# Bias rows, one-hot comparison and group additions redistributed in the edge loop of a two-layer graph network

## The reference, cut to what matters

```python
edge_feat = concatenate([x[src], x[dst], edge_attr], axis=-1)   # 20000 x 1088
h = mish(edge_feat @ W1 + b1)                                   # 20000 x 512
messages = mish(h @ W2 + b2)                                    # 20000 x 512
agg = segment_sum(messages, dst, num_segments=1250)
```

## Time and profile before

| | us |
|---|---|
| runs (3) | 1095.49, 1094.32, 1094.78 |
| median | 1094.78 |
| profiled execution, its own time | 1094.15 |
| its span | 1092.3 |
| busy: PE / weight loads / VectorE / ScalarE / GpSimd | 1033.1 / 871.1 / 861.9 / 884.3 / 724.6 |
| granted TensorE clock, mean | 0.986 |
| edge loop, from the first `z1` behind the node products to the last message | about 370 to 1020 |

### The profile page before, as it was taken

How to read it: one execution, slowest core, us unless ns; L and a number is a source line. 1 busy time by engine, 2 the same in 40 slices (tenths; PEclk the granted TensorE clock), 3 DMA queues, 4 the chain that set the end, 5 groups by cost and what they waited for, 6 DMA issues and landing times.

```text
span 1092.3 us, 18562 instructions
## 1 busy us (share of the span) xinstructions
PE 1033.1 (95%) x5629; PEld 871.1 (80%) x5630; DVE 861.9 (79%) x1500; ACT 884.3 (81%) x1077; POOL 724.6 (66%) x626
## 2 busy tenths in 40 slices
PE   3558999999999999999999999999999999999997
PEld 1226889998889888888888888888888888888796
DVE  7998536635526389999999999999999999999686
ACT  6985735624503799999999999999999999999584
POOL 6875438745255587777777777777777777760227
PEclk8889999999999999999999999999999999999999
DMA  2005962674276387766676666667766666761002
GB/s 106 9 1 139 181 222 73 212 242 149 77 240 116 94 177 163 162 161 139 136 147 139 139 141 146 136 141 141 147 137 138 144 146 134 142 133 39 1 1 95
DMA packets 82914, 141.63 MB, mean 130 GB/s; under 512 B 11115, under 2 KB 39020, under 8 KB 82742
## 3 DMA queue, kind: packets, MB, share of 16 engines
q0 software_dynamic: 38048, 87.58, 40.1%
q1 hardware_dynamic: 44822, 53.52, 15.3%
HBM read 115.42 MB, written 20.39 MB: 124 GB/s over the span
## 4 chain that ended last, share of the span: by engine, by line
PE 85%; DVE 7%; ACT 2%; issue 2%; POOL 1%; DMA 1%; DVEq 1%; ACTq 0%; POOLq 0%
PE banks L1149 12%; PE banks L1150 12%; PE banks L1154 12%; PE banks L1047 10%; PE banks L1181 7%; PE banks L1131 7%; PE banks L1124 6%; PE banks L1091 5%; PE banks L965 4%; PE banks L1112 4%; DVE edge_counts L1823 2%; PE banks L1244 2%; DVE key_onehot L1762 1%; PE banks L1020 1%; PE banks L1147 1%
## 5 line engine op out<-in xcount | busy, mean ns | idle before, releaser
L798 POOL DMA_INDIRECT gather_pq<-q_table,dst x157 | 326.1, 2077 | 57.2 <-issue 47.5
L790 POOL DMA_INDIRECT gather_pq<-p_table,src x157 | 174.8, 1113 | 117.7 <-PE banks L1131 66.7
L1149 PE MATMUL banks<-w_lo,h_hi 128*128 128x512 f32 x620 | 242.0, 390 | 0.0
L1150 PE MATMUL banks<-w_hi,h_hi 128*128 128x512 f32 x620 | 241.8, 390 | 0.0
L1154 PE MATMUL banks<-w_hi,h_lo 128*128 128x512 f32 x620 | 166.0, 389 | 0.0
L1154 PEld LDWEIGHTS banks<-w_hi,h_lo 128*128 128x128 f32 x620 | 116.4, 188 | 24.4
L1150 PEld LDWEIGHTS banks<-w_hi,h_hi 128*128 128x128 f32 x620 | 116.4, 188 | 23.8
L1149 PEld LDWEIGHTS banks<-w_lo,h_hi 128*128 128x128 f32 x620 | 116.4, 188 | 23.3 <-issue 0.7
L2131 DVE SCALAR_TENSOR_TENSOR h_full<-mish_work,banks 128x512 f32<-128x512 f32 (+1 forms) x154 | 98.4, 681 | 45.1 <-ACT mish_work L1465 40.8
L2156 DVE SCALAR_TENSOR_TENSOR message<-mish_work,banks 128x1024 f32<-128x1024 f32 x78 | 95.3, 1222 | 8.4 <-ACT mish_work L1489 0.3
L1124 PE MATMUL banks<-ident,gather_pq 128*128 128x128 f32 x628 | 96.5, 275 | 1.4 <-DVE h_full L2131 0.8
(11 more groups left out here) (274 smaller groups left out, 2607.6 us busy)
## 6 DMA issues: line engine op xcount, KB each, us to landing
edge_attr<-in_edge_attr_t SPq DMA_DIRECT2D x20, 256.0 KB, 2.8
attr_high<-edge_attr_hi SPq DMA_DIRECT2D x40, 128.0 KB, 2.2
attr_low<-edge_attr_lo SPq DMA_DIRECT2D x40, 128.0 KB, 1.8
edge_attr_parts<-attr_high SPq DMA_DIRECT2D x79, 64.0 KB
edge_attr_parts<-attr_low SPq DMA_DIRECT2D x79, 64.0 KB
x_nodes<-h_hi POOLq DMA_DIRECT2D x10, 256.0 KB, 14.9
x_nodes<-h_lo POOLq DMA_DIRECT2D x10, 256.0 KB, 7.9
p_table<-p_stage SPq DMA_DIRECT2D x10, 256.0 KB, 2.0
```

Of the source, the lines that this page charges most:

```text
L790: nc.gpsimd.indirect_dma_start(GP[:, 2 * j + k, :], None, p_tab[:, :], bass.IndirectOffsetOnAxis(ap=SRC[:, 2 * s + k:2 * s + k + 1], axis= ...
L798: nc.gpsimd.indirect_dma_start(GP[:, 2 * j + k, :], None, q_tab[:, :], bass.IndirectOffsetOnAxis(ap=DST[:, 2 * s + k:2 * s + k + 1], axis= ...
L1149: pe.matmul(at, h_high(s, j)[:, c, e], W2_LO[:, c, :], start=False, stop=False, skip_group_check=True)
L1150: pe.matmul(at, h_high(s, j)[:, c, e], W2_HI[:, c, :], start=False, stop=False, skip_group_check=True)
```

## The change

1. `b2_second_tile` of ScalarE is gone. In odd steps VectorE's `b2_rows` writes the row into both banks of the step with one copy of 128x1024; in even steps it writes the first bank as before, and TensorE adds the row in the second by the product with ones. In odd steps TensorE adds none. TensorE waits on one semaphore, counted once a step, ahead of k = 0.
2. `hots1` makes both one-hots with one `tensor_tensor` of 128x2x128 in place of two `tensor_scalar` of 128x128.
3. Of a group's two additions, the one to the lowest tile stays at the end of the even step; the one to the next tile moves to the following odd step, behind `full1` and ahead of `hi2`. `load_range` moves from the end of the even step to a place behind `message` in the odd step.

The order of VectorE in an odd step s is then: `full1(s)` twice, `group_next`, `hi2`, `hi1`, `lo2`, `message`, `load_range`, `hots1`, `b2_rows` (both banks), `lo1`.

```diff
--- before.py
+++ after.py
@@ -416,7 +416,7 @@
         z1_done, a_exp, a_sq, a_ln, a_r, h_hi, h_lo = (sem(n) for n in
             ("z1_done", "a_exp", "a_sq", "a_ln", "a_r", "h_hi", "h_lo"))
         h_full = [sem(f"h_full_{h}") for h in range(2)]
-        z2_done, b2_in, b2_first, b2_second = (sem(n) for n in ("z2_done", "b2_row_in", "b2_in_first_tile", "b2_in_second_tile"))
+        z2_done, b2_in, b2_in_rows = (sem(n) for n in ("z2_done", "b2_row_in", "b2_written"))
         b_exp, b_sq, b_ln, b_r, msg_full, msg_hi, msg_lo = (sem(n) for n in
             ("b_exp", "b_sq", "b_ln", "b_r", "msg_full", "msg_hi", "msg_lo"))
         u_bias, u_exp, u_cut, u_sq, u_ln, u_r, u_ready = (sem(n) for n in
@@ -1140,10 +1140,8 @@
                         pe.wait_ge(up_moved, BLOCKS * KD)
                     pe.wait_ge(h_hi, s + 1)
                 if after(s, 2) and k == 0:
-                    pe.wait_ge(b2_first, s - 1)
-                elif after(s, 2) and j == 0:
-                    pe.wait_ge(b2_second, s)
-                else:
+                    pe.wait_ge(b2_in_rows, s - 1)
+                elif not after(s, 2) or j == 0:
                     pe.matmul(at, ONES_R[:, :], B2_R[:, :], start=True, stop=False, skip_group_check=True)
                 for c in range(KD):
                     pe.matmul(at, h_high(s, j)[:, c, e], W2_LO[:, c, :], start=False, stop=False, skip_group_check=True)
@@ -1488,9 +1486,6 @@
                 act.wait_ge(b_ln, s + 1)
                 nc.scalar.activation(z2_work(s), z2_work(s), ACT.Exp, scale=-1.0).then_inc(b_r, 1)
 
-            def b2_second_tile(s, j):
-                nc.scalar.copy(Z2[:, 2 * j + 1, :], B2_ROW[:, 0, :]).then_inc(b2_second, 2)
-
             def edge_step(s, j):
 
                 if live(s):
@@ -1503,9 +1498,6 @@
                     inv1(s)
                 if live(s - 2):
                     sq2(s - 2)
-                if j == 1 and after(s, 3) and live(s - 1) and tiles(s - 1) == 2:
-                    b2_second_tile(s - 1, 1 - j)
-                if live(s - 2):
                     log2(s - 2)
                 if live(s - 2):
                     inv2(s - 2)
@@ -1527,7 +1519,6 @@
                             log1(s)
                         if n == first + 3:
                             inv1(s)
-            act.wait_ge(b2_in, 16)
             for s in range(2, 4):
                 edge_step(s, s % 2)
             with act.Fori(2, LAST - 1) as i:
@@ -1681,13 +1672,15 @@
             def node_tile(nt):
                 return AGG[:, bass.ds(nt, 1), :].rearrange("p o d -> p (o d)")
 
-            def add_sums(n, row, bank):
-
-                next_tile = dve.snap(range_regs[n][R_NEXT], min_val=0, max_val=NT - 1)
-                for nt, where in ((low_tile(n), FROM_LOW), (next_tile, BELOW_LOW)):
-                    at = node_tile(nt)
-                    ins = nc.vector.scalar_tensor_tensor(at, bank, where[:, bass.ds(row, 1)], at, ALU.mult, ALU.add)
-                return ins
+            def add_low(n, row, bank):
+
+                at = node_tile(low_tile(n))
+                nc.vector.scalar_tensor_tensor(at, bank, FROM_LOW[:, bass.ds(row, 1)], at, ALU.mult, ALU.add)
+
+            def add_next(n, row, bank):
+
+                at = node_tile(dve.snap(range_regs[n][R_NEXT], min_val=0, max_val=NT - 1))
+                return nc.vector.scalar_tensor_tensor(at, bank, BELOW_LOW[:, bass.ds(row, 1)], at, ALU.mult, ALU.add)
 
             def sums_extra(n, rel, tile, hots, bank, added):
 
@@ -2147,7 +2140,10 @@
 
             def hots1(s, j):
 
-                make_hots([ONEHOT[:, j, k, :] for k in range(2)], REL_G, 2 * s).then_inc(hot_ready, 1)
+                wide = [P, 2, P]
+                nc.vector.tensor_tensor(ONEHOT[:, j, :, :], IOTA[:, 0:P].rearrange("p (o k) -> p o k", o=1).broadcast_to(wide),
+                                        REL_G[:, bass.ds(2 * s, 2)].rearrange("p (t o) -> p t o", o=1).broadcast_to(wide),
+                                        ALU.is_equal).then_inc(hot_ready, 1)
 
             def message(s, j):
                 dve.wait_ge(b_r, s + 1)
@@ -2155,9 +2151,12 @@
                     dve.wait_ge(msg_lo, s)
                 nc.vector.scalar_tensor_tensor(MSG[:, :, :], EB[:, :, :], -0.5, z2_out(s, j), ALU.add, ALU.mult).then_inc(msg_full, 1)
 
-            def b2_first_tile(s, j):
+            def b2_rows(s, j):
                 dve.wait_ge(msg_full, s - 1)
-                nc.vector.tensor_copy(Z2[:, 2 * j, :], B2_ROW[:, 0, :]).then_inc(b2_first, 1)
+                if j == 1:
+                    nc.vector.tensor_copy(Z2[:, 2:4, :], B2_ROW[:, :, :].broadcast_to([P, 2, DIM])).then_inc(b2_in_rows, 1)
+                else:
+                    nc.vector.tensor_copy(Z2[:, 0, :], B2_ROW[:, 0, :]).then_inc(b2_in_rows, 1)
 
             def hi2(s):
                 dve.wait_ge(msg_full, s + 1)
@@ -2169,30 +2168,34 @@
                 dve.wait_ge(msg_hi, s + 1)
                 nc.vector.tensor_tensor(MSG_LO[:, :, :], MSG[:, :, :], MSG_HI[:, :, :].bitcast(F32), ALU.subtract).then_inc(msg_lo, 1)
 
-            def add_group(s, n, group, bank):
-
+            def group_low(s, n, group, bank):
 
                 wait_extras()
                 dve.wait_ge(agg_done, SUMS1 + group)
                 dve.wait_ge(seg_done, s + 1)
-                add_sums(n, group, bank).then_inc(agg_done, 1)
+                add_low(n, group, bank)
+
+            def group_next(s, group):
+
+                add_next(0, group, SEG[:, 0, :]).then_inc(agg_done, 1)
+                more_of(s, 0, group + 1)
+
+            def add_group(s, n, group, bank):
+
+
+                group_low(s, n, group, bank)
+                add_next(n, group, bank).then_inc(agg_done, 1)
 
             def more_of(s, n, added):
                 sums_extra(n, REL_G, 2 * s, [XHOT_R[:, k, :] for k in range(tiles(s))], SEG[:, 1, :], SUMS1 + added)
-
-            def sums1(s, group, last):
-
-                if last:
-                    add_group(s, 0, group, SEG[:, 0, :])
-                    more_of(s, 0, group + 1)
-                else:
-                    more_of(s, 0, group)
 
             def edge_step(s, j, i):
 
                 if live(s):
                     for h in range(2):
                         full1(s, h)
+                if j == 1 and live(s - 4):
+                    group_next(s - 4, i - 2)
                 if live(s - 3):
                     hi2(s - 3)
                 if live(s):
@@ -2201,16 +2204,19 @@
                     lo2(s - 3)
                 if live(s - 2):
                     message(s - 2, j)
+                if j == 1 and live(s - 3):
+                    load_range(0, i - 1)
                 if live(s - 2):
                     hots1(s - 2, j)
                     if live(s):
-                        b2_first_tile(s, j)
+                        b2_rows(s, j)
                 if live(s):
                     lo1(s, j)
                 if live(s - 3):
-                    sums1(s - 3, i - 2 + j, j == 0)
-                if live(s - 2) and j == 0:
-                    load_range(0, i - 1)
+                    if j == 0:
+                        group_low(s - 3, 0, i - 2, SEG[:, 0, :])
+                    else:
+                        more_of(s - 3, 0, i - 1)
 
             dve.wait_ge(q_stored, TABLE_STORED)
             dve.wait_ge(b2_in, 16)
@@ -2224,6 +2230,8 @@
                 edge_step(s, s % 2, s // 2)
 
 
+            group_next(FINAL - 3, EDGE_GROUPS - 3)
+            load_range(0, EDGE_GROUPS - 2)
             hi2(FINAL - 2)
             lo2(FINAL - 2)
             more_of(FINAL - 2, 0, EDGE_GROUPS - 2)
```

## The result

The changed kernel takes 1110.11 us in the median of 4 runs (1109.61 to 1110.61), against 1095.02 us for the kernel before (1094.32 to 1095.49). The ratio is 1.0138, with a 95% interval of 1.0121 to 1.0156: slower by 15.1 us. The forecast was 1113.3, range 1107 to 1124. The profiled execution took 1110.61 us, its span 1108.8, that is 16.5 more than before.

The account below looks back on a forecast made before the run. With three engines nearly full, the wait ending last bounds the kernel; the cycle through them was to grow from 16.73 to 17.23 us a pair, 37 x 0.50 = 18.5 us on 1094.78: 1113.3 us, range 1107 to 1124.

Parts of the forecast that it names:

- What bounds the kernel: Edge loop: three engines nearly full; second addition makes a 0.29 us gap at even `z1`; bias row has 0.13 us slack.
- TensorE's row product moved, ScalarE's copy gone: Edge loop: product only moves from odd to even step, ScalarE's 0.58 us copy only gives slack; both valued 0.
- The second addition behind `full1`: VectorE, odd step: `full1` starts 0.56 us earlier, but the addition puts 0.67 us ahead of `hi2` and what follows.
- Register load in its new place: VectorE, odd step: the load is covered by `message` and costs 0; exposed in full, at most 0.82 us.
- Rival B: VectorE, odd step: register load or branch is exposed, 0.3 us a pair on top of the forecast, 1124 us; chance 0.10.
- One comparison: VectorE's one-hots: one operation takes 0.32 us instead of 0.39, saving 0.07 us a step.
- Both rows by VectorE: VectorE, odd step: copy of 1024 columns into PSUM takes 1.22 us, 0.53 more, all ahead of TensorE's wait.
- rival C: Bias-row copy of 1024 columns takes 0.69 us, so no change: cycle 16.70 us, time 1093.7 us; chance 0.05.
- The cycle: Edge loop, odd `z1` through ScalarE, VectorE and `z2(odd, 1, 0)` to next odd `z1`: 17.23 us a pair against 16.73.
- The gap of 0.29 us as a gain of 0.29: TensorE, even `z1`: the idle gap behind `full1` closes, a gain of 0.29 us a pair.
- rival D: Edge loop: faster, only the closed gap counts, 37 x 0.29 = 10.7 us less, 1084.1 us; chance 0.08.
- What is late next: Behind the wait on the rows: `lo1` and `exp2` stay in time; odd VectorE step holds 8.1 us, next `full1` some 8.2 later.

Follow-up runs that it names:

- split_only: Kernel before with only the second addition moved behind the odd `full1` and `load_range` behind `message`: 1094.96 us, ratio 0.9999.
- rows_only: Kernel before with VectorE copying both bias rows in odd steps and TensorE adding the second in even ones; one-hots and additions unchanged: 1101.35 us, ratio 1.0046.
- row_first_three_engines: Changed kernel without the two-row copy (ScalarE keeps its copy), single bias row ahead of the one-hots: 1091.29 us, ratio 0.9965 to the kernel before.
- one_comparison_only: Kernel before with only the new `hots1`, one tensor_tensor for both one-hots: 1096.02 us, ratio 1.0014.
- split_and_comparison: Changed kernel with bias rows as before: split additions and one comparison, without the two-row copy: 1094.53 us, ratio 0.9996 to the kernel before.

## Why the prediction was right, point by point

- **What bounds the kernel**: right. The gap at the even `z1` was made by the additions (split_only removes it), and the slack of 0.13 us at the bias row was the next limit: split_only moves the gap there, 37 times as before.
- **TensorE's row product moved, ScalarE's copy gone, both at 0**: right for the changed kernel, where ScalarE idled 0.70 us ahead of `exp1` in odd steps. The product's 0 holds only because the path left the additions: with them in their old place it was worth 0.22 (rows_only).
- **The second addition behind `full1`**: from `full1` to `hi2` 1.87 us in place of 1.20, so 0.67 as forecast. `full1` came 0.03 behind ScalarE, where I had 0.05.
- **Register load in its new place, 0**: right. From `message` to the one-hots 1.14 us, as before. Rival B, more of it exposed, didn't occur.
- **One comparison**: 0.42 us by itself and 0.33 to the next; forecast 0.408 and 0.32.
- **Both rows by VectorE**: the copy of 1024 columns took 1.220 us in the mean of 38; the upper bound, 1.22, was taken. It runs at the rate of the 512 columns into PSUM (0.687) and not at that of the 1024 within SBUF (0.691). With this rival C falls. Of the two places in the Trainium skill (VectorE: DVE Perf Modes) this trace agrees with the section Why PSUM operands drop a tier, 1× for fp32; the table's "≤2×" is a bound that the copy doesn't reach.
- **The cycle**: 17.23 forecast, 17.15 measured. Term by term, in the order of the forecast, the trace has 2.25, 5.07, 0.03, 5.53 (4.87 and 0.67 together), 0.33, 1.22, a last signal of 0.06 and 0.12 in turn, and 2.63: 17.12 and 17.18 in turn. The signal, 0.03 longer in the mean than the 0.06 forecast, nearly offsets what the others are short; the last term is the difference. From the first weights of `z2(odd, 1, 0)` to the next odd `z1` I took 2.72 us; behind a gap it is 718.29-715.66 = 2.63. Behind the gap the second weight load follows the first 0.11 later (715.66 to 715.77), without a gap 0.23 (706.92 to 707.15). 37 pairs make 37 x 0.41 = 15.2 us, against 15.1 between the medians and 16.5 between the two spans. The 3.2 us by which 1113.3 is above 1110.1 are about this term (0.09 a pair, 37 x 0.09 = 3.3).
- **The gap of 0.29 us as a gain of 0.29**: wrong in size, without harm to the sum, which didn't use it; rival D did. The kernel with no gap at all has a pair of 16.64, so the gap cost only 0.10, and D should have read 37 x 0.10 = 3.7 us less, 1091.1. That row_first_three_engines measures 1091.29 is no second proof, since the 16.64 is its own; it shows that the pairs account for the time. The step that failed is "without the gap TensorE's own work is 16.44": behind the gap the first four weight loads took 0.42 us in place of 0.58, and the odd `z1` that follows came 8.06 later, where the kernel without gaps has 724.09-715.88 = 8.21. The row of the products shows the same place, first in the kernel before, then in row_first_three_engines:

```profile
700.65 1.07 PE L1154 MATMUL banks<-w_hi,h_lo 128*128 128x512 f32 x4
701.58 0.66 PE L1124 MATMUL banks<-ident,gather_pq 128*128 128x128 f32 x4
701.99 0.36 PE L1131 MATMUL banks<-edge_attr_parts,we_hi 128*128 128x256 f32 x1
```

```profile
715.20 1.07 PE L1154 MATMUL banks<-w_hi,h_lo 128*128 128x512 f32 x4
716.11 0.60 PE L1124 MATMUL banks<-ident,gather_pq 128*128 128x128 f32 x4
716.46 0.36 PE L1131 MATMUL banks<-edge_attr_parts,we_hi 128*128 128x256 f32 x1
```

Without a gap the weights of `z1` are loaded 0.23 ahead of their product (715.88 and 716.11); behind the gap both start at 701.58. So 0.29 idle in the weight loads came to 1.34-1.26 = 0.08 in the products: the rest was lead that they had over them. The same holds for the new gap: forecast 0.79, 0.65 in the weight loads, 17.15-16.64 = 0.51 in the pair.
- **What is late next**: the forecast had the next `full1` some 8.2 us behind the odd one, "full, but not beyond". It came 8.31 behind (708.46 to 716.77), because a `full1` right behind `lo1` starts 1.32 later and not 1.13. That is 0.13 behind ScalarE's `inv1`, and harmless: its first half is done long before the odd `z1` at 718.29.

## What to carry to other kernels

When three engines are nearly full, look for the second tightest wait before removing the first: here it was 0.13 us behind, at an instruction that the same change made 0.53 later. Work is cheap or dear by its place in the queue and not by its length (0.35 us ahead of the rows cost 10.3 us in all, behind them nothing), so put what another engine waits for first and let the long copy stand in the step that has the slack. Measure a gap's worth by the period of the loop with and without it, not by the idle time in the weight loads.

## What was not expected

- An idle time of 0.29 us in the weight loads was worth 0.10 us of time; one of 0.65 was worth 0.51.
- At the turn of TensorE's hardware loop, `z1` had idle time in three kernels and then started 1.95 to 2.20 us behind the end of `lo1`; in the loop's other pair of steps, with the same work, it had none. What fills these 2 us is open.
- A VectorE operation that waits for the end of the one just ahead of it started 1.25 us behind that one's start, where unconnected neighbours have 1.14: the wait costs 0.11 us there. From `lo2` to `message` it is 1.32 in all kernels (719.98 to 721.30), so the cost isn't the same everywhere.
- The cast `hi2`, untouched by any edit, takes about 0.1 us longer in odd steps of some kernels (half of them in split_only, all in one_comparison_only and split_and_comparison) and not in the changed kernel; where the split has used up the row's slack, this reaches the time. Its cause is open.
- One `tensor_tensor` for two `tensor_scalar` alone freed 0.06 us of VectorE a step and gained nothing; the 1.3 us by which the median rose are close to the noise.
